# Attention and recurrent kernel on one core: one tile of values moved into the first unit, the second batch's sums of squares two quarters later, its shift added by ScalarE

## The reference

```python
xn = _rms_norm(x, g_norm) * (1.0 + scale) + shift      # scale, shift = emb @ W_emb + b_emb
q, k, v = xn @ W_qkv                                   # 16 heads of 32
q, k = _rms_norm(q, g_q), _rms_norm(k, g_k)
attn = softmax(einsum(q, k) * 32 ** -0.5)
x = x + (o + o @ W_out)                                # o = attn @ v
x = x + GRU(cond, x)                                   # 512 steps, one after the other
x = x + causal_conv_4_taps(x, cond)
x = x + causal_conv_4_taps(x, cond) + b
```

## Time and profile before

| | us |
|---|---|
| median of three runs | 2110.72 |
| lowest and highest | 2109.24, 2111.89 |
| the profiled execution's own time | 2109.71 |
| its span, first to last instruction | 2107.9 |
| PE busy | 2069.3 (98%) |
| DVE busy | 1285.2 (61%) |
| ACT busy | 1192.0 (57%) |
| POOL busy | 642.3 (30%) |

### The profile page before, as it was taken

The page is one execution under the profiler, slowest core; times in us unless marked ns, Lnnn a source line. Parts: engine busy times, 40 slices in busy tenths (PEclk is TensorE's granted clock), DMA queues, the critical chain, the costliest instruction groups (busy, mean ns, idle before and its releaser), DMA issues.

```text
span 2107.9 us, 181496 instructions
## 1 busy us (share of the span) xinstructions
PE 2069.3 (98%) x77848; PEld 1597.7 (76%) x77848; DVE 1285.2 (61%) x6158; ACT 1192.0 (57%) x5995; POOL 642.3 (30%) x1030
## 2 busy tenths in 40 slices
PE   8999999999999999999999999999999999999998
PEld 2222222222499999999999999999999999998887
DVE  4344445444366666666666666666666666666666
ACT  3445544443256666666666666666666666666665
POOL 0355547444112222222222222222222222222223
PEclk9999999999999999999999999999999999999999
DMA  6000000011222222221222221222122212210001
GB/s 260 1 1 1 1 1 1 1 55 37 50 51 55 52 52 55 53 54 49 70 58 55 54 53 51 57 60 66 49 59 51 56 49 60 68 31 11 5 8 20
DMA packets 218227, 96.05 MB, mean 46 GB/s; under 512 B 170232, under 2 KB 213624, under 8 KB 217464
## 3 DMA queue, kind: packets, MB, share of 16 engines
q1 hardware_dynamic: 217176, 92.00, 16.8%
q10 hardware_dynamic: 928, 2.65, 0.3%
HBM read 26.30 MB, written 12.58 MB: 18 GB/s over the span
## 4 chain that ended last, share of the span: by engine, by line
PE 70%; DVE 2%; issue 0%; DMA 0%; ACT 0%; SPq 0%; DVEq 0%
PE ps L1257 64%; PE ps L1290 4%; PE ps L1298 2%; DVE arena L1079 2%; DVE arena L1097 0%; DMA arena<-arena 0%; DVE arena L1092 0%; DVE arena L1085 0%; DVE arena L977 0%; ACT arena L1226 0%; SPq L1000 0%; DVE seq L1115 0%; DVE arena L1163 0%; DVE arena L1175 0%; DVE arena L1170 0%
## 5 line engine op out<-in xcount | busy, mean ns | idle before, releaser
L1257 PE MATMUL ps<-whh,arena 128*4 128x128 f32 (+1 forms) x65568 | 1449.4, 246 | 13.2 <-issue 1.6
L1257 PEld LDWEIGHTS ps<-whh,arena 128*4 128x4 f32 x65568 | 1312.7, 87 | 89.8 <-DVE arena L1097 24.0
L1079 DVE STREAM_TRANSPOSE arena<-ps 128x64 f32<-128x64 f32 x2048 | 446.6, 284 | 312.0 <-PE ps L1257 258.4
L1215 ACT ACTIVATE arena<-arena 128x8 f32<-128x8 f32 x1024 | 216.2, 211 | 589.3 <-DVE arena L1079 589.0
L455 DVE TENSOR_REDUCE top<-ps 128x2 f32<-128x1024 f32 x128 | 150.8, 1220 | 243.7 <-PE ps L722 243.7
L1190 ACT ACTIVATE ps<-arena 128x128 f32<-128x128 f32 x1026 | 288.9, 282 | 0.5 <-PEq L212 0.4
L1097 DVE TENSOR_TENSOR_SCAN arena<-arena 128x24 f32<-128x24 f32 x1024 | 193.2, 189 | 156.0 <-ACT arena L1226 156.0
L1085 DVE STREAM_TRANSPOSE arena<-ps 128x64 f32<-128x64 f32 x1024 | 257.2, 251 | 7.7 <-PE ps L1257 2.4
L610 PE MATMUL ps<-arena 128*32 128x512 f32 x2048 | 242.9, 596 | 2.7 <-ACT arena L383 2.7
L361 ACT ACTIVATE arena<-ps 128x1024 f32<-128x1024 f32 x128 | 124.1, 1021 | 212.4 <-PE ps L798 212.4
L971 POOL TENSOR_TENSOR arena<-tap,arena 128x128 f32<-128x128 f32 x252 | 101.8, 414 | 426.3 <-DVE seq L1115 426.3
(11 more groups left out here) (105 smaller groups left out, 1271.3 us busy)
## 6 DMA issues: line engine op xcount, KB each, us to landing
arena<-arena SPq DMA_DIRECT2D x216, 114.0 KB, 2.2
arena<-arena SPq DMA_DIRECT2D x112, 128.0 KB
arena<-seq SPq DMA_DIRECT2D x224, 55.0 KB
arena<-gi_d SPq DMA_DIRECT2D x248, 32.0 KB
gi_d<-arena SPq DMA_DIRECT2D x96, 57.0 KB
out<-seq SPq DMA_DIRECT2D x13, 256.0 KB, 2.6
seq<-in_x SPq DMA_DIRECT2D x3, 1024.0 KB, 15.6
whh<-in_w_hh SPq DMA_DIRECT2D x1, 3072.0 KB, 21.0
```

The source lines that it names most:

```text
L1079: e.transpose(trn[:, h, q].rearrange("p (i c s) -> p c i s", c=2, s=2)[:, :, :, 0], bank[RN[h]][:, 64 * q:64 * q + 64].rearrange("p (c i) ...
L1215: e.activation(r_d0[:, h].rearrange("p (i s) -> p i s", s=2)[:, :, 1], trn[:, h, 0, 0:2 * NH].rearrange("p (i s) -> p i s", s=2)[:, :, 0], ...
L1257: last = e.matmul(bank[dst[h]][32 * G:32 * G + B, 0:n], hv, wv[:, k, gates, G, 64 * h:64 * h + 64], start=False, stop=k2 == 1 and k == C - ...
```

## The change

Three things change; the computed result stays the same, and no transfer is added or moved.

1. **A tile of values.** `value_tile(-1, 0)` leaves the list ahead of the loop and goes into unit 0, in pieces of one, one and two chunks. `value_tile(-1, 1)`, in unit 0 already, moves one place later. Ahead of the loop, `scores(0, 2)` is put in the middle of `value_tile(-2, 0)`, and `scores(0, 3)` ahead of `value_tile(-2, 1)`. ACT's copies of the two tiles, and the waits on them, move along.
2. **The second batch's sums of squares.** In unit 1, `sums_x(1)` goes from the first quarter (after `shifted(1, 0)`) to the third, where `norm(1, 3)` was; `norm(1, 3)` goes to the fourth quarter, between `weigh` and `shifted(1, 3)`. ACT's `rms_x(1)` and DVE's `scale_x(1)` move along; `scale_x(1)` now comes after `norm(1, 3)`, at the end of unit 1's turn on DVE.
3. **The shift.** POOL's `add_shift(1)` is taken out, and ACT does the four chunks at the start of unit 2, after `tops(2)`. `project(0, 4)` waits for each chunk by itself rather than for all four.

The units 5 and 9, which do the same for the third and fourth batch, stay as they were.

```diff
@@ POOL
-                    if has_x(n):
+                    if has_x(n) and n > 1:
                         add_shift(n // 4 + 1)
@@ ACT
+                def shift_x(b):
+                    for c in range(C):
+                        e.wait_ge(d_xn, C * b + c + 1)
+                        e.activation(xnT[:, c], xnT[:, c], ACT.Identity, bias=modT[:, 1, c, b:b + 1]).then_inc(g_xn, 1)
...
                 for n in range(NS):
                     tops(n)
+                    if n == 2:
+                        shift_x(1)
...
                         rms(0, n + 2)
+                    if n == 1:
+                        rms_x(1)
                     exponentials(n, 2)
...
                     if n == 0:
+                        values(-1, 0)
+                    exponentials(n, 3)
+                    if n == 0:
                         values(-1, 1)
-                    exponentials(n, 3)
@@ DVE
-                    if has_x(n):
+                    if has_x(n) and n > 1:
                         scale_x(n // 4 + 1)
...
                         norm(1, n + 2)
+                    if n == 1:
+                        scale_x(1)
@@ PE, waits
+                        if n in (0, C) and s == 0:
+                            e.wait_ge(g_xn, n + k + 1)
...
                 def norm(s, n):
-                    if s:
+                    if s and n == 3:
+                        e.wait_ge(a_rx, 2 * 1 + 1)
+                    elif s:
                         e.wait_ge(a_ln[0], n + 1)
@@ PE, ahead of the loop
-                value_tile(-2, 0, range(C))
+                value_tile(-2, 0, range(0, 2))
                 scores(0, 2)
+                value_tile(-2, 0, range(2, C))
                 norm(1, 1)
+                scores(0, 3)
                 value_tile(-2, 1, range(C))
-                scores(0, 3)
-                value_tile(-1, 0, range(C))
                 turn_tops(0)
@@ PE, the loop
+                    if n == 0:
+                        value_tile(-1, 0, range(0, 1))
                     scores(n + 1, 2)
                     weigh_late(n, 2)
+                    if n == 0:
+                        value_tile(-1, 0, range(1, 2))
                     tile_x(n, 0, range(0, 1))
-                    norm(1, n + 2)
+                    if n == 1:
+                        sums_x(1)
+                    else:
+                        norm(1, n + 2)
                     shifted(n, 2)
                     if n == 0:
-                        value_tile(-1, 1, range(0, 2))
+                        value_tile(-1, 0, range(2, 4))
                     tile_x(n, 0, range(1, 4))
                     scores(n + 1, 3)
                     weigh_late(n, 3)
                     if n == 0:
-                        value_tile(-1, 1, range(2, 4))
+                        value_tile(-1, 1, range(0, 2))
+                    if n == 1:
+                        norm(1, n + 2)
                     tile_x(n, 1, range(0, 2))
                     shifted(n, 3)
+                    if n == 0:
+                        value_tile(-1, 1, range(2, 4))
                     tile_x(n, 1, range(2, 4))
                     turn_tops(n + 1)
```

More of the change, by code:

```diff
@@ L380, in _ @@
                 rms_x(0)
-                for c in range(C):
-                    e.wait_ge(d_xn, c + 1)
-                    e.activation(xnT[:, c], xnT[:, c], ACT.Identity, bias=modT[:, 1, c, 0:1]).then_inc(g_xn, 1)
+                shift_x(0)
                 keep(0, 0)
@@ L393, in _ @@
                 values(-2, 1)
-                values(-1, 0)
                 for n in range(NS):
                     tops(n)
+                    if n == 2:
+                        shift_x(1)
                     if has_v(n - 1) and n:
@@ L615, in sums_x @@
                         e.wait_ge(d_const, 4)
+                    elif b == 1:
+                        e.wait_ge(a_ln[0], 4)
                     else:
@@ L631, in project @@
                                 e.wait_ge(l_qk[c], 16)
-                            if c == 0 and b:
+                            if c == 0 and b > 1:
                                 e.wait_ge(g_xn, C * b + C)
@@ L638, in project @@
                                 free(e, n - 3, s, n)
-                        if n == 0 and s == 0:
-                            e.wait_ge(g_xn, k + 1)
+                        if n in (0, C) and s == 0:
+                            e.wait_ge(g_xn, n + k + 1)
                         last = product(bank[PQ + s], wqk[:, c, s, k], xnT[:, k], k == 0, k == C - 1)
@@ L645, in free @@
                 def free(e, m, i, n):
-                    if i == 1 and m in (-1, 0):
-                        e.wait_ge(a_v, 2 if m else TB)
+                    if m in (-1, 0):
+                        e.wait_ge(a_v, (TB if i else TB - 1) if m == 0 else i + 1)
                     elif m >= -2 and has_v(m):
@@ L678, in value_tile @@
                                 e.wait_ge(l_v, 16)
-                            if n == -1 and i == 0:
-                                e.wait_ge(a_v, 1)
-                            elif n == -1:
-                                e.wait_ge(a_sq[1], 3)
+                            if n == -1:
+                                e.wait_ge(a_sq[i], 3)
                             else:
@@ L818, in sums @@
                     e.wait_ge(a_top, min(n + 2, NS))
-                    if has_x(n + 1):
+                    if has_x(n + 1) and n:
                         e.wait_ge(a_rx, 2 * ((n + 1) // 4 + 1) + 1)
```

## The result

The changed kernel takes 2136.61 us (median of 4 runs, 2135.33 to 2137.95) against 2110.32 for the kernel before (4 runs beside them): a ratio of 1.0119 [1.0107, 1.0131]. It is 26 us slower. The forecast was 2106.8 with a range up to 2113.0, so both the sign and the size were wrong.

What follows compares the result with a forecast made beforehand. PE, busy 98% of the span, was taken as the bound, with 8.7 us in three waits for ACT and slow clock behind them. Terms summed to -3.9 us on the 2110.7 median: 2106.8, whole range 2105.0 to 2113.0.

Steps and rivals of the forecast that it cites:

- a shift there carries to the end: Behind `shifted(2, 0)` both kernels have the same lists and PE no wait for ACT, so time differences stay unchanged.
- the one place that could turn the sum: End of unit 1: DVE's fourth `scale_x(1)` operation meets POOL's add; assumed to go first, 0 us, otherwise 5.6.
- rival 1: POOL's add catches DVE's fourth `scale_x(1)` operation, PE idles about 3 us, low clock follows: +5.6, total +1.7; chance 0.36.
- The wait at the first `turn_tops`: Ahead of the loop: PE, free at 46.4, waits for the last maxima and `split` until 47.0: +0.7 us.
- Unit 0: Two tile chunks around `shifted(0, 2)` remove a 0.7 us maxima wait but leave 0.3 waiting for ACT: together -0.4.
- Wait A: PE's 1.77 us wait for ACT before `scores(2, 0)`, covered by two chunks: -1.7, and -1.65 for slow clock behind.
- B: PE's 1.92 us wait for ACT before `scores(2, 3)`: stays, becomes 2.1; with the maxima wait gone -0.5; low clock kept.
- rival 2: The low clock falls elsewhere: none behind B gives -5.6, also behind C or the new wait -2.2; chance 0.17, 0.09 faster.
- The maxima ahead of `shifted(1, 3)`: Last quarter of unit 1: `norm(1, 3)` now stands ahead and covers PE's 0.66 us wait for maxima: -0.66.
- C: PE's 1.68 us wait for ACT before `scores(3, 0)`: stays, 0.1 longer through ACT's `rms(1, 3)`, to 1.8; clock whole.
- The shift: Start of unit 2: ACT takes four 0.7 us operations while idle, nobody waited for POOL's: cost 0, at most 0.7.
- The sum without the collision: All terms in the attention layer, with DVE's fourth operation going ahead of POOL's add: -3.9 us; chance 0.38.

Runs made afterwards that it cites:

- a_p1: The changed kernel with one more instruction, an idle wait, in PE's list far ahead of the GRU loop: 2112.13 us, ratio 1.0002 to the kernel before.
- b_m1: The kernel before, its order kept, with one instruction less in PE's list ahead of the GRU loop (two waits share one): 2139.21 us, ratio 1.0127.
- a_head2: The changed kernel with one more instruction in PE's list right ahead of the GRU's first loop: 2112.13 us, ratio 1.0003 to the kernel before.
- b_m1_in2: b_m1 with one more instruction at the end of the loop's body, so the head is early and the branch at its old place: 2150.14 us, 1.0189.
- b_sums: The kernel before with only the second and third part (sums, norms, shift on ACT), PE's list at its old length: 2115.88 us, ratio 1.0014.
- b_tile: The kernel before with only the first part (tile of values and order ahead of the loop), PE's list at its old length: 2110.75 us, ratio 0.9986.
- a_calm: a_p1 with POOL's third add of unit 1 also waiting until all four operations of scale_x(1) are done: 2105.93 us, ratio 0.9973 to the kernel before.
- b_p1: The kernel before with one instruction more, an idle wait, in PE's list ahead of the GRU: 2112.95 us, ratio 0.9998.
- b_m2: The kernel before with two instructions less in PE's list ahead of the GRU: 2138.39 us, ratio 1.0121.

## Why the prediction was wrong

**The step that failed** is the sentence that both kernels have the same lists behind `shifted(2, 0)`, "so a shift there carries to the end". The lists are the same and the time is not. PE's list ahead is one instruction shorter, the loop's head stands one place early, and the branch back costs about 0.25 us in 81 more of 112 turns: 20.7 us of the 22.6 in the GRU. a_p1 and b_m1 show it from both sides, a_head2 that nothing ahead of the loop's head counts; for the head against the branch speaks b_m1_in2, with the reserve made there. No term or rival stood for it. What the trace of before could have told is that 63% of the span (1321.5 of 2107.9) lies in a loop which a branch of PE closes, with PE busy for 98%; what it could not tell is that one place decides. The number of PE's instructions ahead of the loop can be had without a run.

**The second failure** is the choice in the one place that could turn the sum, "by that row the fourth here goes first too". It did not. The third operation was the last to go; POOL's add, begun 0.17 us behind it, then held DVE's fourth until it was done: 7.03 - 2.73 = 4.3 us, as rival 1 had it. The Trainium skill (SBUF — State Buffer, section Who interferes with whom) has a VectorE operation with two SBUF inputs contend with a GpSimd one that reads SBUF, the shared port pair an exclusive lock, and the order of issue deciding who waits. The trace agrees here, in all four kernels in which the add starts during `scale_x` (the changed one, a_p1 and a_head2 7.03, b_sums 7.02 us). The old `scale_x` was POOL's operation of 512 columns with a scalar, which took 1.99 to 2.9; the add is one of 2048 columns with two tensors. A row of another kind of operation was set above a row of the same kind (L468, held for 2.31 by an add of squares), and that was the wrong way round.

**The terms**, one by one:
- The wait at the first `turn_tops`: 0.7 said, 0.48 measured. The tile itself was added as said.
- Unit 0: the maxima no longer hold `shifted(0, 2)`, as said, and PE's wait for ACT behind it is 0.16 where 0.3 was left.
- Wait A and its low clock: gone, as said. b_tile alone gives -3.0 us, against the terms of its part, 0.7 - 0.4 - 1.7 - 1.65 = -3.05. That the two agree to 0.05 is luck: the interval of the ratio reaches from -4.9 to -1.1, and in b_tile's profiled execution the clock was half behind C too.
- B: 2.1 said, 2.10. The low clock behind it, kept in the forecast, did not come in this execution; a clock term of rival 2, worth 1.7 there. In a_p1, with the same order and the same 2.10, it came.
- The maxima ahead of `shifted(1, 3)`, and C: the wait for the maxima was to go and C to be 1.8. That is what a_p1 shows, with the low clock behind B (no wait; 1.86). In the changed kernel, with the whole clock, PE comes earlier: 2.20 us pass from `shifted(1, 3)` to `turn_tops` (106.95 to 109.15, with 0.16 of waiting for `split`) where 1.28 was said, and C is 1.44. So of the 1.7 of rival 2's clock some 1.15 are won: 6.97 us from the `scores` behind B to the one behind C, against 8.12 in a_p1.
- The shift: 0 said. ACT's last operation waits 3.43 us for DVE's fourth, but only because of the collision; in a_calm nothing waits for it.
- The sum without the collision: -3.9 said, about -5.7 by a_calm's ratio (from -8.0 to -3.2 by its interval), -5.24 in the profiled executions (82.92 against 88.16). Most of the 1.3 us of difference there is B's clock.
- Rival 1's price: 5.6 said, 6.2 measured (a_p1 - a_calm), 6.45 between the profiled executions of the changed kernel and a_calm. PE's idle time of 3 us is as said. What comes behind it, the second half of the maxima and the low clock, was put at 2.6 and is 3.4: `shifted(2, 0)` and its products take 7.39 us (117.85 to 125.24) against 4.00 (113.57 to 117.57). Its total, +1.7 in this execution, was +1.2 up to the `scores` behind `shifted(2, 0)`; and with the loop at a fast place a_p1 measures 1.0002. Had the loop stayed where it was, the time would have been 2111 to 2112, inside the range.

**Open.** Why a head one place early costs 0.25 us is not shown. No more packets of instructions are fetched: the page of every kernel, fast or slow, has the same two rows of instruction queues (packets, MB, share):

```profile
q8 instruction: 47, 0.77, 0.2%
q14 instruction: 76, 0.62, 0.1%
```

The first of them fits PE's list. In the trace its packets stop some 0.5 us behind the first loop's first branch (589.6 and 593.9 above) and come again some 2 us behind its last (1911.2 and 1936.3). In between, from 590 to 1913 us in the kernel before and from 594 to 1939 in the changed one, it brings nothing, and so it is in all thirteen kernels.

The Trainium skill says that a branch whose target is outside the instructions held makes a fetch (Runtime: NRT & Kernel Launch, section Instruction fetch mechanics). That speaks of the right thing, the place of a branch's target. But the trace shows no added fetch. Why 83 to 110 turns are long rather than all or none is open as well, and why the second loop, whose head moved too, is not touched. So is whether a head further ahead becomes fast again.

## What to carry to other kernels

Before a gain of a few microseconds in one stage is forecast, ask whether the edit changes the length of an engine's list ahead of a hot loop. A change of one instruction was worth 25 to 27 us here (the change against a_p1, b_m1 against the kernel before), over six times the gain that was forecast for the order. When a difference sits in code that didn't change, add one idle wait ahead of the loop: one run tells place from order. And compare profiles of several kernels that share a stage before a single execution's clock there is put into a sum: the stretch measured above took 86.80 to 89.55 us with one order and the same three waits.

Where a DVE operation and a POOL one meet in SBUF, take the price of the operation of the same kind and size from the trace, and if the order of issue is within a microsecond, count on the bad case. One wait that puts POOL behind DVE cost nothing and won 6.2 us.

## What the runs showed of the hardware

- The place of a loop's head in PE's list costs time by itself: -1 and -2 instructions give a ratio of 1.0127 and 1.0121, +1 and +16 give 0.9998 and 0.9995. The cost falls in the step with the branch back, about 0.25 us, and not in every turn. The branch's own record has a median of 208 ns in fast and slow kernels; the time passes behind the loop's first instruction (medians of 0.45 and 0.46 us in the changed kernel and b_m1, 0.19 in the kernel before and a_p1).
- Added waits that are already met cost nothing that the runs show in PE's list ahead of the loop: 32 of them in 16 instructions, 0.9995 [0.9984, 1.0007].
- POOL's add, begun while DVE's third of four operations ran, held the fourth for 4.3 us and itself took 4.98 instead of 4.55.
- A wait of 2.10 us (B in the changed kernel) left the clock whole, where waits of 1.77 and 1.92 had brought the low clock in the kernel before. In a_p1 the same wait of 2.10 brought it. A wait of 1.68 (C) left the clock whole in four kernels and brought the low clock in b_m1 and b_p1, and one of 1.77 (A) left it whole in b_m2. The length of the idle time alone doesn't decide.
